# Moving the block-mask step ahead of the weight masking on VectorE, and ahead of the small transfers on GpSimd

## The chip, the cores and the metric

One Trainium2 chip, all 8 cores, each running the same program on its own 2048 of the 16384 tokens. Nothing is exchanged between cores. The time is the device time of the slowest core, in microseconds (us).

## The reference

Two layers follow each other on `x` of shape (2, 8192, 4096):

```python
def _L0_attn_ref(data, weight, mask):
    block_mask = mask.reshape(nb, 32, kb, 32).astype(jnp.float32).sum(axis=(1, 3)) > 0
    elem_mask = jnp.repeat(jnp.repeat(block_mask, 32, axis=0), 32, axis=1)
    return jnp.einsum('bsk,nk->bsn', data, weight * elem_mask)

x = x + _layernorm(_L0_attn_ref(_layernorm(x), L0_attn_weight, L0_attn_mask))
x = x + _layernorm(einsum('bsi,oi->bso', _layernorm(x), sign(L0_ffn_weight)) + bias)
```

Both weights and the integer mask are 4096 x 4096. What this change touches is the block mask: every 32 x 32 block of the mask is summed, and a block of the first weight counts only if its sum is above zero.

## The kernel before

Each core works through its tokens in four chunks of 512 (`c` = 0 to 3), and in each chunk through two layers. A layer is 16 slabs: slab `sl` covers 512 output columns (`nsl = sl // 2`) and half of the contraction (`kh = sl % 2`). For one slab TensorE (PE) runs 64 matmuls of 512 columns (L474), 16 for each of four token tiles. After each odd slab the four accumulated banks are moved out of PSUM (in the first layer of chunk 0 by VectorE, DVE: L528, with statistics in L537).

In chunk 0 the weights come as 32-bit floats and have to be prepared. For each slab `emit_w_load_prep` (L338) makes SyncE (SP) load eight pieces of 512 KB into two alternating buffers `WST` (L364); a piece may be loaded only once the piece two before it has been used. In layer 0 DVE multiplies each piece by the block mask `BTE` into the slab buffer `WSL` (L393); there are two slab buffers. Then SP writes the finished slab, 2 MB, to DRAM for the later chunks (L418), ahead of the loads of the next slab in its queue. The preparation of slab `sl + 1` is issued before the matmuls of slab `sl`, so that the two overlap.

The block mask is built during the same stage, for one `nsl` at a time, in two steps:

- `emit_mask_front(nsl)` (L220), on GpSimd (POOL) alone: four loads of 2 MB of mask rows (L243), and for each a tree of five additions (L258) that leaves column sums. Even `nsl` works in `OS` and `MHI`, odd `nsl` in the two halves of `XP`.
- `emit_mask_tail(nsl)` (L267): ScalarE (ACT) converts the sums to `COLRED` (L280); PE sums over rows with one matmul into `ptB` (L292); DVE compares with zero into `BRT` (L306); PE transposes it in four small pieces (L297); DVE copies the result to `BT` (L310); POOL writes `BT` to DRAM and reads it back, spread over the partitions, into one of two buffers `BTE` (L323, L332).

`front` 0 and 1, `tail` 0 and 1, and `front` 2 and 3 come before the first slab. After that, at each even slab `sl = 2j`, the program issues `tail(j + 2)` and `front(j + 4)`. `tail(j + 2)` waits on POOL for `bte_freed[j]`, the masking of slab `2j + 1`. Every engine runs its own instructions strictly in the order of the program; only semaphores tie the engines together. The lines around the change:

```python
for sl in range(NSL):
    if sl + 1 < NSL:
        nxt = emit_w_load_prep(c, layer, sl + 1)
    ...
    emit_slab_mm(c, layer, sl, ready, su, ev_at, ht_mark, site, ...)
    if c == 0 and layer == 0 and sl % 2 == 0:
        j = sl // 2
        if j + 2 <= 7:
            emit_mask_tail(j + 2, False)
        if j + 4 <= 7:
            emit_mask_front(j + 4)
```

Of the kernel before, what the change touches and what calls it, by code (L numbers as in the profile page):

```python
# [15 lines left out]
BF16 = mybir.dt.bfloat16  # L16
# [21 lines left out]
def build():  # L38
# [16 lines left out]
    with es:  # L55
        def sb(name, shape, dt):
            return es.enter_context(nc.sbuf_tensor(name, shape, dt))
# [11 lines left out]
        BRT = sb("BRT", [4, 512], BF16)  # L69
        BT = sb("BT", [128, 128], BF16)  # L70
# [13 lines left out]
        ptB = es.enter_context(nc.psum_tensor("ptB", [128, 1024], F32))  # L84

        sem = {n: es.enter_context(nc.semaphore(n)) for n in SEMS}
        cnt = {n: 0 for n in SEMS}

        def inc(ins, n, k=1):
            cnt[n] += k  # L90
            ins.then_inc(sem[n], k)
            return (n, cnt[n])

        def wt(eng, marker):
            if marker is None:
                return
            n, v = marker
            if v > 0:
                eng.wait_ge(sem[n], v)

        blk = es.enter_context(nc.Block())
# [9 lines left out]
        bte_freed = {}  # L111
# [6 lines left out]
        @blk.gpsimd  # L118
        def _(g):
            g.dma_start(IDN[:, :], idn_d[:, :]).then_inc(sem["sA"], 16)  # L120
            g.dma_start(P4T[:, :], p4_d[:, :]).then_inc(sem["sA"], 16)
            g.dma_start(ONES1[:, :], ones1_d[:, :]).then_inc(sem["sA"], 16)
            g.dma_start(OS[0:1, :], bias_d[:, :]).then_inc(sem["sA"], 16)
# [96 lines left out]
        def emit_mask_front(nsl):  # L220
# [14 lines left out]
            def _(g):  # L235
# [28 lines left out]
                        cur = tree[:, dst_off:dst_off + dst_n]  # L264
                halv[nsl] = ("vPs", cnt["vPs"])

        def emit_mask_tail(nsl, first):  # L267
            halv = mask_halv
            conv = mask_conv
            par = nsl % 2  # L270
            XPI = XP[:, :].bitcast(I32)
            tree = MHI if par == 0 else XPI[:, 4096:8192]
            fin_base = 3072

            @blk.scalar
            def _(s):
                wt(s, halv[nsl])
                if nsl >= 1:
                    s.wait_ge(sem["vTp"], 5 * (nsl - 1) + 1)
                ins = s.activation(COLRED[:, :],  # L280
                                   tree[:, fin_base:fin_base + 512],
                                   AF.Identity)
                conv[nsl] = inc(ins, "vAs", 1)

            @blk.tensor
            def _(t):
                wt(t, conv[nsl])
                if first:
                    wt(t, bias_ptB_free)
                if nsl >= 1:  # L290
                    t.wait_ge(sem["vMk"], 2 * (nsl - 1) + 1)
                ins = t.matmul(ptB[0:4, 0:512], P4T[:, :], COLRED[:, :],  # L292
                               start=True, stop=True)
                inc(ins, "vTp", 1)
                t.wait_ge(sem["vMk"], 2 * nsl + 1)
                for r in range(4):
                    ins = t.transpose(ptB[:, :].bitcast(BF16)[:, 1024 + r * 4:  # L297
                                                              1028 + r * 4],
                                      BRT[0:4, r * 128:(r + 1) * 128],
                                      IDN[0:4, 0:4])  # L300
                    inc(ins, "vTp", 1)

            @blk.vector
            def _(v):
                v.wait_ge(sem["vTp"], 5 * nsl + 1)
                ins = v.tensor_scalar(BRT[0:4, :], ptB[0:4, 0:512], 0.0, None,  # L306
                                      OP.is_gt)
                inc(ins, "vMk", 1)
                v.wait_ge(sem["vTp"], 5 * nsl + 5)
                ins = v.tensor_copy(BT[:, 16 * nsl:16 * nsl + 16],  # L310
                                    ptB[:, :].bitcast(BF16)[:, 1024:1040])
                inc(ins, "vMk", 1)

            res = {}

            @blk.gpsimd
            def _(g):
                g.wait_ge(sem["vMk"], 2 * nsl + 2)
                g.wait_ge(sem["sB"], cnt["sB"])
                if nsl >= 2:  # L320
                    wt(g, bte_freed[nsl - 2])
                bteb = BTE[nsl % 2]
                g.dma_start(btd_d[:, :], BT[:, 16 * nsl:16 * nsl + 16]  # L323
                            ).then_inc(sem["sB"], 16)
                cnt["sB"] += 16
                g.wait_ge(sem["sB"], cnt["sB"])
                for a in range(4):
                    out_ap = bass.AP(bteb[:, :].tensor, 32 * a * 512,
                                     [[512, 32], [16, 32], [1, 16]])
                    in_ap = bass.AP(btd_d[:, :].tensor, a * 16,  # L330
                                    [[0, 32], [64, 32], [1, 16]])
                    g.dma_start(out_ap, in_ap).then_inc(sem["sB"], 16)  # L332
                    cnt["sB"] += 16
                res["m"] = ("sB", cnt["sB"])

            bte_ready[nsl] = res["m"]
# [469 lines left out]
        for c in range(NCH):  # L806
            t0 = c * TC
            if c == 0:
                emit_p0_part1(0, list(range(NT)), phase="loads")
                emit_mask_front(0)  # L810
                emit_mask_front(1)
                emit_mask_tail(0, True)
                emit_mask_tail(1, False)
                emit_mask_front(2)
                emit_mask_front(3)
                emit_p0_part1(0, list(range(NT)), phase="stats")
            else:
                emit_p0_part1(c, [1, 2, 3])
            p0_norm = emit_p0_part2(c)
            a2_norm = None  # L820

            for layer in range(2):
                ev_at = {}
                site = 1 if layer == 0 else 3
                norm_marks = p0_norm if layer == 0 else a2_norm
                single_pt = (c == 0 and layer == 0)
                te_done = {}
                tr_base = state["tr_groups"]

                def pre_tt(t, tt, _nm=norm_marks, _sp=single_pt, _c=c,  # L830
                           _layer=layer, _te=te_done):
                    extra = []
                    if _c == 0 and _layer == 1 and tt == 0:
                        extra.append(("vMk", 16))
                    for grp in range(2):
                        _te[(tt, grp)] = emit_h_transposes_grp(
                            t, tt, grp, _nm[tt] if grp == 0 else None,
                            _sp, extra if grp == 0 else [])

                def ht_mark(tt, _tb=tr_base):  # L840
                    return ("vTe", _tb + 2 * tt + 2)

                pend = emit_w_load_prep(c, layer, 0)
                for sl in range(NSL):
                    if sl + 1 < NSL:
                        nxt = emit_w_load_prep(c, layer, sl + 1)
                    if layer == 0 and fin_pending[0] is not None:
                        fc, fev = fin_pending[0]
                        if sl == 0:
                            fin_chain[0] = emit_finalize_chain(fc, fev)  # L850
                        elif sl == 1:
                            for ftt in range(NT):
                                emit_finalize_tile(fc, fin_chain[0], ftt)
                            fin_pending[0] = None
                    ready, su = pend
                    emit_slab_mm(c, layer, sl, ready, su, ev_at, ht_mark, site,
                                 pre_tt=pre_tt if sl == 0 else None)
                    if c == 0 and layer == 0 and sl % 2 == 0:
                        j = sl // 2
                        if j + 2 <= 7:  # L860
                            emit_mask_tail(j + 2, False)
                        if j + 4 <= 7:
                            emit_mask_front(j + 4)
                    if layer == 1 and sl == 8 and c + 1 < NCH:
                        emit_p0_part1(c + 1, [0])
                    if sl + 1 < NSL:
                        pend = nxt

                prev_ev[0] = {tt: ev_at[(7, tt)] for tt in range(NT)}

                if layer == 0:
                    a2_norm = emit_a2(c, t0, ev_at)
                else:
                    fin_pending[0] = (c, ev_at)
# [45 lines left out]
```

## Time and profile before

| | us |
|---|---|
| median of two runs | 3415.11 |
| lowest and highest of the two | 3378.73, 3451.49 |
| the profiled execution | 3383.73 |
| its span on the slowest core, core 3 | 3382.2 |
| spans of all cores | 3337.3 to 3382.2 |
| busy in the span: PE, DVE, ACT, POOL | 2033.5, 889.0, 606.0, 356.1 |

The profile is of one execution. Its times count from the first instruction of core 3. The page gives PE a busy share of 60%, but the slices of the span differ: the stage that the change touches, layer 0 of chunk 0, lies between about 220 and 865 us, and there PE is busy a third of the time or a little more. POOL is hardly used after 740 us.

### The profile page before, as it was taken

Reading aid. Unit: us, or ns where it says so; the run is one execution under the profiler, and the core shown is the slowest. Engines: PE = TensorE matmul, PEld = TensorE weight load, DVE = VectorE, ACT = ScalarE, POOL = GpSimd, SP = SyncE. Lnnn points to the kernel's source line nnn. Section 1 sums busy time; section 2 is a strip of 40 time slices with the busy share of each in tenths; the row PEclk is TensorE's granted clock in tenths of the full one; section 3 lists DMA queues with packets and bytes.
Section 4 is the critical chain, followed back from the end, with each engine's and each line's share of the span. In section 5 each row is a group of like instructions: output and inputs, shape, how many; then the busy total and the mean of one; then the engine's idle time right before and its main releaser. Section 6 shows DMA issues by size and latency. Waiting matters only on the chain.

```text
span 3382.2 us, 24252 instructions; the slowest of 8 cores (3337.3 to 3382.2 us)
## 1 busy us (share of the span) xinstructions
PE 2033.5 (60%) x9272; PEld 935.3 (28%) x9272; DVE 889.0 (26%) x1300; ACT 606.0 (18%) x460; POOL 356.1 (11%) x296
## 2 busy tenths in 40 slices
PE   1013333345235545455994899589579966966992
PEld 0011111112112212222442444234234432433441
DVE  0043444434401011024004122410312142022214
ACT  0130000000443232241114200211330030125000
POOL 3554444400000000000000000000000000000000
PEclk9997766678667777777996999889779987986996
DMA  3367766766356666655343344444334444442442
GB/s 125 123 253 216 242 223 238 242 214 221 114 159 189 199 193 200 200 190 175 149 149 129 120 179 156 163 167 156 132 117 164 160 149 174 149 153 74 156 157 107
DMA packets 72947, 573.15 MB, mean 169 GB/s; under 512 B 8800, under 2 KB 8816, under 8 KB 42112
## 3 DMA queue, kind: packets, MB, share of 16 engines
q1 hardware_dynamic: 58752, 444.62, 38.2%
q0 software_dynamic: 14080, 126.97, 11.3%
q8 instruction: 75, 1.23, 0.1%
q14 instruction: 40, 0.33, 0.0%
HBM read 470.86 MB, written 100.70 MB: 169 GB/s over the span
## 4 chain that ended last, share of the span: by engine, by line
PE 37%; DMA 34%; DVE 11%; ACT 11%; issue 4%; POOL 1%; SPq 0%; DVEq 0%; ACTq 0%; POOLq 0%
PE pmm L474 36%; DMA WST<-w1s 13%; DMA WST<-w2s 11%; DVE WSL L393 4%; DMA out<-OS 3%; DMA XS<-x 3%; ACT WSL L407 2%; ACT HS L738 2%; ACT HS L707 2%; DVE OS L786 2%; ACT HT L214 1%; DMA WSL<-c1m 1%; DVE BNST L593 1%; DMA OS<-mask 1%; PE ptA L204 1%
## 5 line engine op out<-in xcount | busy, mean ns | idle before, releaser
L474 PE MATMUL pmm<-WSL,HT 128*128 128x512 bf16 x8192 | 1904.8, 397 | 648.9 <-ACT WSL L407 260.1
L474 PEld LDWEIGHTS pmm<-WSL,HT 128*128 128x128 bf16 x8192 | 826.7, 102 | 1717.8 <-issue 839.2
L530 DVE TENSOR_TENSOR ARAW<-pmm,BIASF 128x512 bf16<-128x512 f32 x128 | 88.6, 692 | 1021.0 <-PE pmm L474 1021.0
L393 DVE TENSOR_TENSOR WSL<-WST,BTE 128x1024 bf16<-128x1024 f32 x128 | 234.3, 1849 | 348.1 <-DMA WST<-w1s 332.4
L204 PE MATMUL ptA<-IDN,HS 128*128 128x128 bf16 x576 | 64.7, 301 | 367.3 <-ACT HS L738 235.5
L511 DVE BATCH_NORM_STATS2 BNST<-ARAW 128x6 f32<-128x512 bf16 x96 | 59.3, 681 | 544.2 <-ACT ARAW L501 544.2
L407 ACT ACTIVATE WSL<-WST 128x1024 bf16<-128x1024 f32 x128 | 133.4, 1054 | 166.4 <-DMA WST<-w2s 166.2
L204 PEld LDWEIGHTS ptA<-IDN,HS 128*128 128x128 bf16 x576 | 56.6, 139 | 380.7 <-issue 380.0
L258 POOL TENSOR_TENSOR XP<-XP 128x2048 int32<-128x2048 int32 (+4 forms) x80 | 137.7, 1721 | 104.9 <-DMA XP<-mask 97.2
L675 POOL DMA_DIRECT2D XS<-x x32 | 22.4, 699 | 1129.8 <-DVE XP L700 1080.9
L562 POOL DMA_DIRECT2D XS<-x x24 | 12.7, 528 | 1161.9 <-ACT HS L627 1093.9
L214 ACT ACTIVATE HT<-ptA 128x2048 bf16<-128x2048 bf16 x36 | 67.6, 1877 | 274.5 <-PE ptA L204 274.5
L280 ACT ACT_TABLE_LOAD x8 | 10.3, 1283 | 555.3 <-POOL XP L258 283.7
L501 ACT ACTIVATE ARAW<-pmm 128x512 bf16<-128x512 f32 x96 | 57.3, 597 | 266.9 <-PE pmm L474 153.1
L593 DVE BATCH_NORM_STATS2 BNST<-XS 128x6 f32<-128x512 f32 x128 | 78.4, 679 | 101.5 <-DMA XS<-x 101.5
L501 ACT ACT_TABLE_LOAD x24 | 30.8, 1283 | 403.5 <-PE pmm L474 403.5
L537 DVE BATCH_NORM_STATS2 BNST<-ARAW 128x6 f32<-128x512 bf16 x160 | 98.9, 681 | 4.1
L297 PE MATMUL ptB<-IDN,BRT 4*128 4x4 bf16 x32 | 1.9, 161 | 139.6 <-DVE BRT L306 139.6
L258 POOL TENSOR_TENSOR MHI<-MHI 128x1024 int32<-128x1024 int32 (+1 forms) x64 | 76.1, 1189 | 7.7
L786 DVE SCALAR_TENSOR_TENSOR OS<-XP,AUX,OS 128x4096 f32<-128x4096 bf16 x16 | 71.8, 4485 | 1.7
L292 PE MATMUL ptB<-COLRED,P4T 128*4 128x512 bf16 x8 | 3.4, 430 | 114.0 <-ACT COLRED L280 114.0
L258 POOL TENSOR_TENSOR MHI<-OS 128x2048 int32<-128x2048 int32 x16 | 57.5, 3596 | 111.5 <-DMA OS<-mask 111.5
(57 smaller groups left out, 742.2 us busy)
## 6 DMA issues: line engine op xcount, KB each, us to landing
WSL<-c1m SPq DMA_DIRECT2D x48, 2048.0 KB, 7.9
WSL<-c2m SPq DMA_DIRECT2D x48, 2048.0 KB, 7.8
WST<-w1s SPq DMA_DIRECT2D x128, 512.0 KB, 6.4
WST<-w2s SPq DMA_DIRECT2D x128, 512.0 KB, 4.4
XS<-x POOLq DMA_DIRECT2D x56, 1024.0 KB, 5.5
OS<-mask POOLq DMA_DIRECT2D x16, 2048.0 KB, 10.2
XP<-mask POOLq DMA_DIRECT2D x16, 2048.0 KB, 10.0
c1m<-WSL SPq DMA_DIRECT2D x16, 2048.0 KB, 8.8
```

Of the source, the lines that this page charges most:

```text
L204: ins = t.transpose(pt[:, j * 128:(j + 1) * 128], HS[:, ktg * 128:(ktg + 1) * 128], IDN[:, :])
L214: ins = eng.activation(dst, src, AF.Identity)
L258: ins = g.tensor_tensor(tree[:, dst_off:dst_off + dst_n], a[:, :, 0], a[:, :, 1], op=OP.add)
L393: ins = v.tensor_tensor(dst, src, mk, op=OP.mult)
L407: ins = s.activation(buf[:, j0 * 512:(j0 + KTQ) * 512], WST[(wfirst + q) % 2][:, :], AF.Sign)
L474: ins = t.matmul(acc_bank(use8, nsl, tt), st_ap, mv_ap, start=(kh == 0 and j == 0), stop=(kh == 1 and j == KTS - 1))
L501: ins = s.activation(dst, acc_bank(use8, nsl, tt), AF.Identity)
L530: ins = v.tensor_tensor(dst, acc_bank(use8, nsl, tt), BIASF[:, nsl * 512:(nsl + 1) * 512], op=OP.add)
L537: ins = v.bn_stats(BNST[:, sslot * 48 + nsl * 6: sslot * 48 + (nsl + 1) * 6], ARAW[:, tt * D + nsl * 512: tt * D + (nsl + 1) * 512])
L593: ins = v.bn_stats(bn[:, (hf * 4 + q) * 6: (hf * 4 + q + 1) * 6], xb[:, q * 512:(q + 1) * 512])
L707: ins = s.activation(HS[:, :], XP[:, tt * D:(tt + 1) * D], AF.Square, accum_out=XSQ[:, tt:tt + 1])
L786: ins = v.scalar_tensor_tensor(OS[:, :], XP[:, tt * D:(tt + 1) * D], mrs3, OS[:, :], OP.subtract, OP.add)
```

## The change

The two DVE instructions of the mask tail (the comparison and the copy) become a function of their own, `emit_mask_tail_pre`. At an even slab `sl = 2j` it is now issued first, for `nsl = j + 2`; `emit_mask_front(j + 4)` comes right behind it; both stand ahead of the preparation of slab `sl + 1`. The rest of the tail (ACT, PE, POOL) stays behind the matmuls of slab `sl`. POOL's wait for `bte_freed` is written out as a constant of the same value. No instruction is added or taken away.

```diff
+        def emit_mask_tail_pre(nsl):
+            @blk.vector
+            def _(v):
+                v.wait_ge(sem["vTp"], 5 * nsl + 1)
+                ins = v.tensor_scalar(BRT[0:4, :], ptB[0:4, 0:512], 0.0, None,
+                                      OP.is_gt)
+                inc(ins, "vMk", 1)
+                v.wait_ge(sem["vTp"], 5 * nsl + 5)
+                ins = v.tensor_copy(BT[:, 16 * nsl:16 * nsl + 16],
+                                    ptB[:, :].bitcast(BF16)[:, 1024:1040])
+                inc(ins, "vMk", 1)
+
         def emit_mask_tail(nsl, first):
...
-            @blk.vector
-            def _(v):
-                v.wait_ge(sem["vTp"], 5 * nsl + 1)
-                ins = v.tensor_scalar(BRT[0:4, :], ptB[0:4, 0:512], 0.0, None,
-                                      OP.is_gt)
-                inc(ins, "vMk", 1)
-                v.wait_ge(sem["vTp"], 5 * nsl + 5)
-                ins = v.tensor_copy(BT[:, 16 * nsl:16 * nsl + 16],
-                                    ptB[:, :].bitcast(BF16)[:, 1024:1040])
-                inc(ins, "vMk", 1)
...
                 if nsl >= 2:
-                    wt(g, bte_freed[nsl - 2])
+                    g.wait_ge(sem["vW"], 16 * nsl - 16)
...
                 emit_mask_front(0)
                 emit_mask_front(1)
+                emit_mask_tail_pre(0)
+                emit_mask_tail_pre(1)
                 emit_mask_tail(0, True)
...
                 for sl in range(NSL):
+                    if c == 0 and layer == 0 and sl % 2 == 0:
+                        j = sl // 2
+                        if j + 2 <= 7:
+                            emit_mask_tail_pre(j + 2)
+                        if j + 4 <= 7:
+                            emit_mask_front(j + 4)
                     if sl + 1 < NSL:
                         nxt = emit_w_load_prep(c, layer, sl + 1)
...
-                    if c == 0 and layer == 0 and sl % 2 == 0:
-                        j = sl // 2
-                        if j + 2 <= 7:
-                            emit_mask_tail(j + 2, False)
-                        if j + 4 <= 7:
-                            emit_mask_front(j + 4)
+                    if c == 0 and layer == 0 and sl % 2 == 0 and sl // 2 + 2 <= 7:
+                        emit_mask_tail(sl // 2 + 2, False)
```

How this changes the order on DVE, at the start of the stage. Before, DVE masks slab 0 and slab 1 (eight L393 each), does the mask step of `nsl` 2, and masks slab 2:

```order
L393 TENSOR_TENSOR WSL<-WST,BTE 128x1024 x8
L374 UNCONDITIONAL_BRANCH
L393 TENSOR_TENSOR WSL<-WST,BTE 128x1024 x8
L303 UNCONDITIONAL_BRANCH
L306 TENSOR_SCALAR BRT<-ptB 4x512
L310 COPY BT<-ptB 128x16
L374 UNCONDITIONAL_BRANCH
L393 TENSOR_TENSOR WSL<-WST,BTE 128x1024 x8
```

After the change the same rows of DVE read (line numbers are those of the changed kernel, L394 is the masking, L271 and L275 the mask step):

```order
L394 TENSOR_TENSOR WSL<-WST,BTE 128x1024 x8
L268 UNCONDITIONAL_BRANCH
L271 TENSOR_SCALAR BRT<-ptB 4x512
L275 COPY BT<-ptB 128x16
L375 UNCONDITIONAL_BRANCH
L394 TENSOR_TENSOR WSL<-WST,BTE 128x1024 x8
L375 UNCONDITIONAL_BRANCH
L394 TENSOR_TENSOR WSL<-WST,BTE 128x1024 x8
```

The mask step has moved from behind the masking of slab 1 to ahead of it. The same happens at slabs 3, 5, 7, 9 and 11.

On POOL, before, the end of `front(3)` (its last tree, in `XP`) is followed by the transfers of `tail(2)`, and then by `front(4)`, whose first load goes to `OS`:

```order
L258 TENSOR_TENSOR XP<-XP 128x256
L258 TENSOR_TENSOR XP<-XP 128x128
L316 UNCONDITIONAL_BRANCH
L323 DMA btd<-BT 128x16
L332 DMA BTE<-btd 32x32x16 x4
L234 UNCONDITIONAL_BRANCH
L243 DMA OS<-mask 128x4096
```

After the change, the end of `front(3)` is followed at once by `front(4)`:

```order
L258 TENSOR_TENSOR XP<-XP 128x256
L258 TENSOR_TENSOR XP<-XP 128x128
L234 UNCONDITIONAL_BRANCH
L243 DMA OS<-mask 128x4096
L258 TENSOR_TENSOR MHI<-OS 128x2048
```

and the transfers of `tail(2)` (L324, L333) stand behind the last tree of `front(4)`, ahead of `front(5)`:

```order
L258 TENSOR_TENSOR MHI<-MHI 128x128
L317 UNCONDITIONAL_BRANCH
L324 DMA btd<-BT 128x16
L333 DMA BTE<-btd 32x32x16 x4
L234 UNCONDITIONAL_BRANCH
L243 DMA XP<-mask 128x4096
```

So each `front` from 4 to 7 has moved ahead of one set of small transfers. The order on PE, ACT and SP is as before.

## Rows read from the trace of the kernel before

**Rows 1.** Waits, 300 to 700 us: waiter <- releaser, total us, times, longest us

```profile
DVE WSL L393 <- DMA WST<-w1s: 205.2, 49, 12.2
...
PE ptB L297 <- DVE BRT L306: 124.9, 5, 27.4
...
POOL btd L323 <- DVE BT L310: 46.2, 5, 9.7
```

**Rows 2.** Timeline of DVE around slabs 2 and 3 (start us, duration us, idle before)

```profile
353.29 2.47 DVE L528 CAST ARAW<-pmm 128x512 bf16<-128x512 f32 x4
...
370.56 4.96 DVE L393 TENSOR_TENSOR WSL<-WST,BTE 128x1024 bf16<-128x1024 f32 x2 [12.22 <-DMA WST<-w1s]
...
396.65 0.67 DVE L306 TENSOR_SCALAR BRT<-ptB 4x512 bf16<-4x512 f32 x1
```

**Rows 3.** Timeline of PE: the matmuls of slab 2, and each mask matmul (L292)

```profile
274.21 0.38 PE L292 MATMUL ptB<-COLRED,P4T 128*4 128x512 bf16 x1
...
354.12 15.64 PE L474 MATMUL pmm<-WSL,HT 128*128 128x512 bf16 x64 [36.41 <-DVE ARAW L528]
369.69 0.38 PE L292 MATMUL ptB<-COLRED,P4T 128*4 128x512 bf16 x1
...
461.72 0.38 PE L292 MATMUL ptB<-COLRED,P4T 128*4 128x512 bf16 x1
...
552.72 0.38 PE L292 MATMUL ptB<-COLRED,P4T 128*4 128x512 bf16 x1
...
641.86 0.38 PE L292 MATMUL ptB<-COLRED,P4T 128*4 128x512 bf16 x1
...
713.60 0.38 PE L292 MATMUL ptB<-COLRED,P4T 128*4 128x512 bf16 x1
```

**Rows 4.** Timeline of DVE: first masking instruction of slabs 1, 5, 7

```profile
272.44 1.45 DVE L393 TENSOR_TENSOR WSL<-WST,BTE 128x1024 bf16<-128x1024 f32 x1 [13.96 <-DMA WST<-w1s]
...
459.89 3.86 DVE L393 TENSOR_TENSOR WSL<-WST,BTE 128x1024 bf16<-128x1024 f32 x2 [9.65 <-DMA WST<-w1s]
...
549.64 3.21 DVE L393 TENSOR_TENSOR WSL<-WST,BTE 128x1024 bf16<-128x1024 f32 x2 [9.53 <-DMA WST<-w1s]
```

**Rows 5.** The same for slabs 9 and 11

```profile
639.03 3.58 DVE L393 TENSOR_TENSOR WSL<-WST,BTE 128x1024 bf16<-128x1024 f32 x2 [9.39 <-DMA WST<-w1s]
...
705.89 2.36 DVE L393 TENSOR_TENSOR WSL<-WST,BTE 128x1024 bf16<-128x1024 f32 x2 [4.45 <-DMA WST<-w1s]
```

**Rows 6.** Timeline of PE, then DVE: an undisturbed mask tail

```profile
147.26 0.59 PE L292 MATMUL ptB<-COLRED,P4T 128*4 128x512 bf16 x1 [53.67 <-ACT COLRED L280]
...
149.15 0.17 DVE L310 COPY BT<-ptB 128x16 bf16<-128x16 bf16 x1 [0.52 <-PE ptB L297]
```

**Rows 7.** Timeline of POOL: tail(2), first load and last row of front(4), end of front(7)

```profile
302.24 0.56 POOL L323 DMA_DIRECT2D btd<-BT  x1 [9.73 <-DVE BT L310]
...
315.43 0.57 POOL L243 DMA_DIRECT2D OS<-mask  x1
...
382.75 6.76 POOL L258 TENSOR_TENSOR MHI<-MHI 128x1024 int32<-128x1024 int32 x4
...
646.62 10.69 POOL L258 TENSOR_TENSOR XP<-XP 128x2048 int32<-128x2048 int32 x5 [3.75 <-DMA XP<-mask]
```

**Rows 8.** Timeline of DVE: evictions after slabs 8, 12 and 14

```profile
624.59 2.47 DVE L528 CAST ARAW<-pmm 128x512 bf16<-128x512 f32 x4
...
761.73 2.48 DVE L528 CAST ARAW<-pmm 128x512 bf16<-128x512 f32 x4
...
817.96 2.48 DVE L528 CAST ARAW<-pmm 128x512 bf16<-128x512 f32 x4
```

**Rows 9.** Instructions by line, window 223:665, then window 697:850 (busy us, mean ns)

```profile
L393 DVE TENSOR_TENSOR WSL<-WST,BTE 128x1024 bf16<-128x1024 f32 x80 | 176.1, 2224 | 239.5 <-DMA WST<-w1s 223.9 <-DMA btd<-BT 15.4 <-issue 0.2
...
L393 DVE TENSOR_TENSOR WSL<-WST,BTE 128x1024 bf16<-128x1024 f32 x40 | 48.6, 1225 | 87.0 <-DMA WST<-w1s 87.0
```

**Rows 10.** Stage 370:397 (PE, PEld, DVE, ACT, POOL busy, granted clock, DMA share, GB/s)

```profile
370.00:397.00 27.00, 0.07 (x1) 0.00 (x0) 17.04 (x9) 1.91 (x2) 16.00 (x10) 0.59 0.58 196
```

## The prediction

> **What bounds the kernel now.** The change reaches only layer 0 of chunk 0, so I read the waits of 300 to 700 us first. The largest in time that looks like the change's target is PE's: its transposes of the mask waited 124.9 us for DVE's comparison, up to 27.4 us at a time, and POOL waited 46.2 us for DVE's copy [rows 1]. DVE itself waited 205.2 us for weight pieces [rows 1]. Which of them ends last is seen in the timelines. DVE masks slab 3 until 396.6, and does the comparison at 396.65 [rows 2]; PE had stood ready with its mask matmul since 369.69 [rows 3]. But what PE wants next is the matmuls of slab 3, and these need the masked slab, which is ready at the same 396.6. PE's long wait is thus for the slab, under another name: the comparison costs it about 1 us. The stage is bound by the chain on each weight piece: SP's load, DVE's masking, which frees the buffer, SP's next load. PE and POOL hang beside it.
>
> What the masking costs depends on POOL. Its instruction takes 2224 ns on average while POOL builds trees, 1225 ns without [rows 9]. Three pairs of slabs with a front beside each last from the evictions at 353.29 to those at 624.59, 90.4 us each [rows 2, 8]; a pair without a front lasts 56.2 us, from 761.73 to 817.96 [rows 8]. So a front costs the chain some 34 us, by its loads and its trees together.
>
> **The wait that is added.** DVE's comparison of `nsl` j + 2 now stands ahead of the masking of slab 2j + 1, but it still needs PE's mask matmul, which stands behind all 64 matmuls of slab 2j. Before, DVE masked slab 2j + 1 beside these matmuls; now eight maskings queue behind the comparison, behind them SP's loads from the third piece on (two are in the buffers), and then PE's slab 2j + 1. So DVE may start a slab no sooner than the end of the slab before on PE, plus the tail. I compare that with when it started before. An undisturbed tail goes from the mask matmul's start at 147.26 to the end of the copy at 149.32, 2.06 us, with a matmul of 0.59 us [rows 6]; with the 0.38 us of this stage [rows 3] it is 1.85. The mask matmul's start plus 1.85, less the old first masking:
>
> - slab 1: 274.21 + 1.85 - 272.44 = 3.6 [rows 3, 4]
> - slab 3: 369.69 + 1.85 - 370.56 = 1.0 [rows 2, 3]
> - slab 5: 461.72 + 1.85 - 459.89 = 3.7 [rows 3, 4]
> - slab 7: 552.72 + 1.85 - 549.64 = 4.9 [rows 3, 4]
> - slab 9: 641.86 + 1.85 - 639.03 = 4.7 [rows 3, 5]
> - slab 11: 713.60 + 1.85 - 705.89 = 9.6 [rows 3, 5]
>
> The sum is 27.5 us. The delays are small because the matmuls of a slab take only 15.6 us [rows 3], and the first piece of the next slab arrives late anyway: 12.22 us of idle DVE before slab 3 [rows 2], behind the 2 MB that SP writes back first. At slab 11, where no front runs, it arrives sooner and the new wait shows more. A delayed first masking delays the third load by as much, and so the whole chain; nothing in the stage catches up, since DVE is idle waiting for pieces. Slab 9 will be free of fronts after the change (below), and would then look like slab 11: 5 us more. Against that, of the 13.2 us on slabs 1 to 7 a part is given back: POOL goes on while DVE stands still, and a front's work in that time costs no masking. At 34 us of cost in 90 us that is about 5. I keep 27.5.
>
> **The waits that go.** PE has done its transposes early and starts odd slabs at the last masking, some 1 us sooner. This is worth nothing: the next slab on the chain waits for DVE and the loads, not for PE.
>
> POOL no longer waits for the comparison at the end of a front. `front(4)` starts at the end of `front(3)`, 302.24 - 9.73 = 292.5, and not at 315.43 [rows 7]: 23 us sooner. With the other waits, POOL's 46.2 us in all [rows 1], `front(7)` ends near 610 and not at 657.3 [rows 7]. What is late next? The transfers of `tail(2)`, now behind `front(4)`: 292.5, plus that front's 389.5 - 315.4 = 74.1, plus 13.2 for the transfers (302.24 to 315.43), is 380 [rows 7]. DVE needs `BTE` for slab 4 after 396.65 [rows 2], so 17 us remain, and later fronts gain distance. The `vW` wait in the tail is past by then. ACT's conversions have their sums earlier than before. So POOL is early and nobody waits for it: the direct gain is nothing.
>
> What its earliness does to the chain is not shown by the trace, and I bound it. If a front costs its 34 us whenever it runs, nothing changes; four fronts stay four fronts, only packed closer and over sooner. If instead a pair costs 90.4 us in POOL's company however dense that is, 46 us less of company saves 46 x 34 / 90.4 = 17 us. On the other side, today's fronts stand in step with the slabs: their quiet end falls on the end of the odd slabs. Today one tree of a front's four falls into the pause before an odd slab's first piece (DVE idle from 358.3 to 370.56 [rows 2]) and meets no masking. A front lengthens the 16 maskings of its pair by 2224 - 1225 = 1.0 us on average [rows 9], 16 us in all. If the fourth tree meets maskings like the other three, that grows by a third, 5 us a front, 21 us for four. I take 0, the middle of -17 and +21.
>
> The Trainium skill ("SBUF — State Buffer", Who interferes with whom) states a rule that speaks against the packing: a VectorE instruction with two inputs in SBUF and a GpSimd instruction that reads SBUF block each other for the whole instruction. The trace agrees that the masking, which is such an instruction, grows from 1225 to 2224 ns [rows 9]. By that rule the sum would lean to its upper end of +21; by the pairs' additive cost it stays at 0.
>
> **Sum.** 3383.7 (the profiled execution) + 27.5 - 0 + 0 = 3411; leaning a little on the refund of 5 us, I say 3408. The median of the two runs shown, 3415, lies between two values 73 us apart, and the profiled execution is close to the lower; I count from the profile. The change is +0.7%, inside the 2% (68 us) that a measurement of this kernel can tell from no change.
>
> **Rivals.**
>
> - Packing pays. POOL is done 46 us sooner and the slabs behind it run at 56 us a pair, while the new waits vanish beneath late pieces: with POOL loading masks without a pause, first pieces may arrive at every odd slab as late as at slab 3, where the wait is 1.0 us. Then 6 x 1 - 17 gives -11: 3373. Against it: at slabs 9 and 11 no front runs, and their 4.7 and 9.6 us are certain.
> - PE's old wait was real. If the 124.9 us were on the path, five waits of 25 us would go: 3383.7 - 125 = 3259. Against it stand [rows 2, 3]: the end of the wait coincides with the end of the slab's masking.
> - PE's clock, the one on the slower side. DVE now waits for each even slab's matmuls, so their speed is on the path. They took 15.6 us even after 36.41 us of idle [rows 3]. While PE idles the granted clock is 0.59, near the lower level of 1.2 GHz [rows 10]. If the bursts stayed there, 64 matmuls would take between 0.59 / 0.38 = 1.55 times as long (the mask matmul in either state [rows 3, 6]) and twice, 8.6 to 15.6 us more. Six slabs add 52 to 94 us to the 27.5: about +100, 3484. It decides (over 2%) as soon as the bursts take over 22 us. Against it: PE's pattern of bursts and pauses is nearly unchanged, and the bursts of this stage are fast. The Trainium skill ("TensorE: Matmul & The Clock Gate", Loop structure matters more than you think) says that a long wait for data sends PE to its lower clock. The idle row agrees [rows 10], but the burst behind such a wait is fast here [rows 3], which keeps this rival's chance low.
> - Late mask. If `front(4)`, in the company of slabs 1 and 2 and of the write-back, took 30 us more than 74, `BTE` would come 13 us after slab 4 wants it, and DVE would stand. Once behind, POOL's period sets the pace: up to four times 13, +80 with the 27.5, 3463. Against it: the 17 us of room, and that POOL gains on the slabs each time.
>
> **Chances.** The waits as summed: 0.70, with a range of its own from 3390 (27.5 - 17, less 5) to 3437 (27.5 + 21 + 5). Packing pays: 0.17. PE's old wait real, faster by over 2%: 0.03. The clock: 0.05. Late mask: 0.05, of which half is beyond 2%. So faster 0.03, same 0.89, slower 0.08. The range goes from 3373, the packing rival, to 3445, the upper end with the spread of the runs added.
>
> **What would show it.** In the changed profile: DVE idle before the first masking of slabs 1, 3, 5, 7, 9 and 11 is put down to PE's small matmuls or DVE's copy, 16 to 19 us after the last slab's end; PE's wait at the transposes is gone, and an equal one stands before the odd slabs' matmuls; `front(7)` ends near 610; the last eviction of layer 0 comes some 27 us later. A pair of slabs with a front much under 90 us would prove the packing rival; a first masking that waits for BTE, the late mask; bursts above 20 us, the clock. The forecast is wrong if the layer ends earlier than before or over 60 us later.

## The result, and the profile after

| | before | after |
|---|---|---|
| median, us (runs) | 3377.34 (23) | 3395.46 (24) |
| lowest, us | 3362.97 | 3384.51 |
| ratio of the runs, 95% interval | | 1.0075 [1.0054, 1.0096] |
| profiled execution: span of the slowest core | 3382.2 (core 3) | 3391.5 (core 1) |
| mean of the eight spans | 3354.7 | 3378.6 |

The change costs 0.75%, 25 us, and the interval keeps clear of no change. In some executions the cores of one die show a lower granted clock and end later; the medians above include them, the ratios leave them out, and so the ratio stands for means of about 3373 and 3398 us, 25 apart, where the medians lie 18 apart. The slowest cores of the two profiled executions differ by 9 us only, the means of all cores by 24. Spans of the cores lie up to 45 us apart in one of these two, so where a few microseconds matter, the following reads all eight. The interval is 0.2% to either side: a difference well under the 2% that the prediction named can be told.

First the waits between 300 and 700 us in the kernel after (waiter <- releaser, total us, times, longest), against [rows 1]:

```profile
DVE WSL L394 <- DMA WST<-w1s: 186.3, 46, 14.8
PE pmm L475 <- DVE WSL L394: 155.6, 5, 41.8
...
POOL btd L324 <- DVE WSL L394: 86.1, 3, 58.6
...
DVE BRT L271 <- PE ptB L304: 48.8, 4, 12.9
...
PE ptB L309 <- DVE BRT L271: 3.7, 4, 0.9
```

PE's 124.9 us at the mask transposes have become 3.7. What stands there instead is a longer wait for the masked slab, 155.6 us, which was hidden under the other name before. DVE has a wait that it did not have: 48.8 us for PE's mask matmul here, and 78.3 us over the whole stage, by the group of its line between 220 and 900 us (busy us, mean ns, idle before):

```profile
L271 DVE TENSOR_SCALAR BRT<-ptB 4x512 bf16<-4x512 f32 x6 | 4.1, 679 | 78.3 <-PE ptB L304 78.3
```

At slab 11, where no front runs, the timelines of DVE and of PE show the step whole. They answer to the last rows of [rows 3, 5].

```profile
720.39 2.48 DVE L529 CAST ARAW<-pmm 128x512 bf16<-128x512 f32 x4
722.98 2.47 DVE L538 BATCH_NORM_STATS2 BNST<-ARAW 128x6 f32<-128x512 bf16 x4
738.55 0.68 DVE L271 TENSOR_SCALAR BRT<-ptB 4x512 bf16<-4x512 f32 x1 [13.10 <-PE ptB L304]
739.74 0.17 DVE L275 COPY BT<-ptB 128x16 bf16<-128x16 bf16 x1 [0.51 <-PE ptB L309]
740.05 2.36 DVE L394 TENSOR_TENSOR WSL<-WST,BTE 128x1024 bf16<-128x1024 f32 x2
```

```profile
721.22 16.91 PE L475 MATMUL pmm<-WSL,HT 128*128 128x512 bf16 x64 [15.85 <-DVE ARAW L529]
738.06 0.38 PE L304 MATMUL ptB<-COLRED,P4T 128*4 128x512 bf16 x1
739.37 0.23 PE L309 MATMUL ptB<-IDN,BRT 4*128 4x4 bf16 x4 [0.93 <-DVE BRT L271]
760.28 16.16 PE L475 MATMUL pmm<-WSL,HT 128*128 128x512 bf16 x64 [20.67 <-DVE WSL L394]
```

DVE has masked slab 10 and moved the banks of slab 9 out of PSUM (the eviction) by 725.5, and stands for 13.1 us, until PE has finished the 64 matmuls of slab 10. Then two maskings follow each other without a gap (2.36 us for both): both pieces had been lying in their buffers. From the eviction's start to the first masking it is 19.7 us. Before, that eviction began at 696.38 (timeline of DVE of the kernel before),

```profile
696.38 2.48 DVE L528 CAST ARAW<-pmm 128x512 bf16<-128x512 f32 x4
```

and the first masking of slab 11 at 705.89 [rows 5], 9.5 us later. That is the 10 us of one slab.

POOL's side, from its timeline (end of `front(3)`, start of `front(4)`, transfers of `tail(2)`, end of `front(7)`), against [rows 7]:

```profile
283.61 9.70 POOL L258 TENSOR_TENSOR XP<-XP 128x2048 int32<-128x2048 int32 x5 [7.73 <-DMA XP<-mask]
293.87 0.55 POOL L243 DMA_DIRECT2D OS<-mask  x1 [0.56 <-POOL XP L258]
...
363.25 0.56 POOL L324 DMA_DIRECT2D btd<-BT  x1 [0.74 <-POOL MHI L258]
...
596.74 0.40 POOL L258 TENSOR_TENSOR XP<-XP 128x128 int32<-128x128 int32 x1 [0.43 <-POOL XP L258]
620.77 0.57 POOL L324 DMA_DIRECT2D btd<-BT  x1 [23.63 <-DVE WSL L394]
```

`front(7)` ends at 597.1 instead of 657.3, 60 us sooner, and then POOL stands for 23.6 us until slab 7 is masked and `BTE` may be overwritten. In this profile nobody waits for POOL.

The time by slab says where the 25 us arise. Below is when each slab is masked (the start of SP's write-back of it, read from the eight timelines and averaged, us); the runs beside it are those of the next section:

| kernel | 0 | 1 | 3 | 5 | 7 | 8 | 9 | 10 | 11 | 15 |
|---|---|---|---|---|---|---|---|---|---|---|
| before | 259 | 299 | 392 | 482 | 573 | 621 | 662 | 695 | 724 | 847 |
| after | 258 | 310 | 419 | 516 | 610 | 641 | 679 | 710 | 749 | 873 |
| dve_only | 262 | 302 | 399 | 493 | 587 | 638 | 679 | 711 | 749 | 877 |
| pool_only | 257 | 308 | 419 | 516 | 607 | 638 | 668 | 701 | 731 | 856 |
| pe_early | 260 | 313 | 422 | 518 | 607 | 638 | 669 | 701 | 731 | 855 |
| nofront_before | 262 | 303 | 367 | 429 | 490 | 522 | 552 | 585 | 615 | 740 |
| nofront_after | 257 | 299 | 369 | 439 | 509 | 541 | 579 | 612 | 650 | 776 |
| nofront_pe_early | 258 | 299 | 362 | 424 | 485 | 517 | 548 | 580 | 610 | 734 |

Each line is one profiled execution, so that differences of a few us between lines decide nothing alone. The kernel after ends the layer 26 us late, and nearly all of that is still there at the end of the program (24 us in the mean span). On the way it is not spread evenly. Up to slab 7 it falls behind by 37 us, gets 22 of them back by slab 10, and loses 10 again at slab 11.

### The profile page after: what moved, and what is told of

It reads as the page before. It is cut to its first block, busy times and chain, and to the rows that moved or that the text cites. A ratio compares the mean times of both kernels' runs of the same rounds, so it can differ in the third digit from the quotient of the medians.

```text
span 3391.5 us, 24252 instructions; the slowest of 8 cores (3359.4 to 3391.5 us)
## 1 busy us (share of the span) xinstructions
PE 2032.9 (60%) x9272; PEld 934.7 (28%) x9272; DVE 885.5 (26%) x1300; ACT 606.4 (18%) x460; POOL 347.9 (10%) x296
## 4 chain that ended last, share of the span: by engine, by line
PE 40%; DMA 31%; DVE 11%; ACT 11%; issue 4%; POOL 1%; SPq 0%; DVEq 0%; ACTq 0%; POOLq 0%
PE pmm L475 39%; DMA WST<-w1s 12%; DMA WST<-w2s 11%; DVE WSL L394 4%; DMA out<-OS 3%; ACT WSL L408 2%; DMA XS<-x 2%; ACT HS L739 2%; ACT HS L708 2%; DVE OS L787 2%; ACT HT L214 1%; DVE BNST L594 1%; DMA OS<-mask 1%; DMA WSL<-c1m 1%; PE ptA L204 1%
## 5 line engine op out<-in xcount | busy, mean ns | idle before, releaser
L394 DVE TENSOR_TENSOR WSL<-WST,BTE 128x1024 bf16<-128x1024 f32 x128 | 229.2, 1806 | 311.8 <-DMA WST<-w1s 310.4
L594 DVE BATCH_NORM_STATS2 BNST<-XS 128x6 f32<-128x512 f32 x128 | 78.3, 679 | 97.4 <-DMA XS<-x 97.4
L784 DVE TENSOR_SCALAR OS<-ARAW,RS 128x4096 f32<-128x4096 bf16 x16 | 37.7, 2353 | 122.2 <-DMA out<-OS 121.3
```

The costliest lines, as they stand in the source:

```text
L394: ins = v.tensor_tensor(dst, src, mk, op=OP.mult)
L594: ins = v.bn_stats(bn[:, (hf * 4 + q) * 6: (hf * 4 + q + 1) * 6], xb[:, q * 512:(q + 1) * 512])
```

## The experiments

Two theories. **W**: DVE's wait for the end of PE's even slab is the whole cost. **P**: the cost is the closer packing of POOL's fronts, and the wait lies beneath late pieces anyway. The ratios are all to the kernel before, timed beside each group of runs; a range in brackets is its 95% interval.

### One half each

`dve_only` is the changed kernel with `front` back behind the tail:

```diff
-                        if j + 4 <= 7:
-                            emit_mask_front(j + 4)
...
                         emit_mask_tail(sl // 2 + 2, False)
+                    if c == 0 and layer == 0 and sl % 2 == 0 and sl // 2 + 4 <= 7:
+                        emit_mask_front(sl // 2 + 4)
```

> Only the DVE half of the change: the mask step stands ahead of the masking of the odd slab, while POOL keeps its old order (the transfers of tail(j+2), then front(j+4)). Theory W (the added wait on PE is the whole cost): about +27 us over the kernel before, 0.8%, and a layer 0 of chunk 0 that ends 25 to 30 us later. Theory P (the packing of the fronts is the cost, and the wait lies beneath late pieces): under +8 us. In both, POOL waits for the masking of the odd slab (bte_freed) where it waited for the copy before, so its fronts do not start sooner.

`pool_only` is the kernel before with the two calls exchanged:

```diff
-                        if j + 2 <= 7:
-                            emit_mask_tail(j + 2, False)
                         if j + 4 <= 7:
                             emit_mask_front(j + 4)
+                        if j + 2 <= 7:
+                            emit_mask_tail(j + 2, False)
```

> Only the POOL half: front(j+4) is issued ahead of the transfers of tail(j+2); DVE and PE keep the order of before. Theory W: within 10 us of the kernel before, since four fronts cost the same wherever they run; front(7) ends about 45 us sooner. Theory P: +20 us or more. A third theory, that packing pays and is hidden in the full change by the waits: -10 to -17 us.

Measured: the DVE half 1.0061 [1.0038, 1.0085], 21 us; the POOL half 1.0006 [0.9981, 1.0031], 2 us. Together they make 0.67%, against 0.75% for the whole. The interval of `pool_only`, -6 to +11 us, keeps clear of P's +20 and of the -10 to -17 of the third theory, that packing pays; both fall. `front(7)` ended at 607.7 there, 50 us sooner than before. In the profile of `dve_only` the new wait has the size that it has in the whole change:

```profile
L271 DVE TENSOR_SCALAR BRT<-ptB 4x512 bf16<-4x512 f32 x6 | 4.1, 679 | 77.1 <-PE ptB L304 77.1
```

The table shows what packing does. In `pool_only` slab 7 is 34 us later than before, since most of the four fronts have run by then, and by slab 9 it is only 6 us later. The layer ends 9 us late in this one profile; the timing shows 2 us, and 9 lies inside its interval.

### The fronts taken away

Both kernels of this pair leave out the mask loads and trees of `front` 4 to 7, so that what they compute for the columns of `nsl` 4 to 7 is not the reference; they serve this comparison alone.

```diff
         def emit_mask_front(nsl):
             halv = mask_halv
+            if nsl >= 4:
+                halv[nsl] = ("vPs", cnt["vPs"])
+                return
```

> The kernel before without the mask loads and trees of column groups 4 to 7 (the block mask of these groups is then that of stale sums; the tails still run). Additive cost of 34 us a front: about -136 us, 4%. If the masking of a slab were not slowed by POOL and its loads, 0. Pairs of slabs then last about 56 us from slab 2 on.

> The changed kernel without the mask loads and trees of column groups 4 to 7, as in the run before this one. With no front in the way the first pieces of an odd slab land some 9.5 us before DVE may take them, at five slabs, and 3.6 us at slab 1: theory W expects +50 us against the kernel before without those fronts, twice what the full change costs. Theory P (packing costs) expects 0 to 10, since there is nothing left to pack.

Measured against the kernel before: 0.9636 [0.9603, 0.967] without the fronts, 0.973 [0.9693, 0.9767] with the change on top. The difference is 0.94% of 3390, 32 us, from four runs and three; with the two intervals taken as independent, 15 to 49 us. (A later expectation quotes 34 us, the difference of the medians.) The four fronts cost 3.64%, 123 us or 31 each, where I had 34. P's 0 to 10 us is missed; whether the change costs more without fronts than with them, 32 us against 25, the timing can't tell. W's 50 us is too high, though. The rows show why: the evictions behind the masking of slabs 8 and 10 stand in the timeline of DVE in `nofront_after`,

```profile
539.52 1.88 DVE L532 CAST ARAW<-pmm 128x512 bf16<-128x512 f32 x3
...
608.99 2.48 DVE L532 CAST ARAW<-pmm 128x512 bf16<-128x512 f32 x4
```

some 70 us apart (the first line shows the last three of four copies; the first began at 538.9), where a pair takes 61 to 63 us in `nofront_before` by the table. From slab 1 to slab 15 the change adds 477 - 437 = 40 us in these profiles: 8 us at each of five waits, not the 9.6 of slab 11, which I had taken over for all of them. Slab 1 costs nothing, where I had 3.6.

### The wait shortened

The clean test of W leaves DVE's new order alone and lets PE answer sooner. PE's part of the mask tail goes inside the even slab: the mask matmul after the first token tile, the transposes after the second. ACT's conversion is issued ahead of the slab. (Shown are the new PE function and its call; the old places of both parts are switched off.)

```diff
+        def pe_mask(t, nsl, step):
+            if step == 0:
+                wt(t, mask_conv[nsl])
+                t.wait_ge(sem["vMk"], 2 * (nsl - 1) + 1)
+                ins = t.matmul(ptB[0:4, 0:512], P4T[:, :], COLRED[:, :],
+                               start=True, stop=True)
+                inc(ins, "vTp", 1)
+            else:
+                t.wait_ge(sem["vMk"], 2 * nsl + 1)
...
                     if kh == 1 and tt < NT - 1:
                         mm_marks[tt] = inc(ins, "vMM", 1)
+                    if mask_nsl is not None and tt < 2:
+                        pe_mask(t, mask_nsl, tt)
```

> The changed kernel, with PE's part of the mask tail moved into the even slab: the mask matmul after the first 16 of its 64 matmuls, the transposes after the second 16. DVE's mask step can then end some 8 us after the slab starts, before the first piece of the next slab lands (9.5 to 17 us). Theory W: the whole 25 us vanish, and the time is that of the POOL half alone, within 0.3% of the kernel before. If the cost lay in anything else of DVE's new order than the end of PE's matmuls, +0.6 to 0.8% stays. POOL's waits for the masking of the odd slab stay as in the changed kernel.

> The DVE half alone (POOL in its old order), with PE's mask matmul and transposes inside the even slab, after 16 and 32 of its 64 matmuls. The DVE half alone took 0.61% more. Theory W: that goes back to 0, within 0.3% of the kernel before. If 0.4% or more stays, DVE's wait for the end of PE's slab isn't what the half costs.

> The changed kernel without the mask loads and trees of column groups 4 to 7 (stale sums there, the tails still run), with PE's part of the tail inside the even slab. Without fronts the change cost 34 us, 0.9%. Theory W: with the early PE part the time is that of the kernel before without those fronts, 0.964 of the kernel before, within 0.3%; layer 0 of chunk 0 ends as early, its pairs of slabs at 60 to 61 us and not at 70.

| | without early PE part | with it |
|---|---|---|
| whole change | 1.0075 [1.0054, 1.0096] | 1.0021 [0.9987, 1.0055] |
| DVE half | 1.0061 [1.0038, 1.0085] | 1.0017 [0.9983, 1.0051] |
| change without fronts (against 0.9636 before) | 0.973 [0.9693, 0.9767] | 0.9643 [0.9581, 0.9705] |

In each case what stays can't be told from nothing. The drop itself, the two intervals taken as independent, is 0.54% with an uncertainty of 0.40 in the first line, 0.44 with 0.41 in the second and 0.87 with 0.72 in the third: each is clear of nothing by little, and the three agree. In `pe_early` DVE's idle time before the comparison falls from 78.3 to 14.2 us:

```profile
L271 DVE TENSOR_SCALAR BRT<-ptB 4x512 bf16<-4x512 f32 x6 | 4.1, 679 | 14.2 <-PE ptB L296 14.2
```

while the copy behind it now waits 18.5 us for PE's transposes, where it waited 3.1: together 33 us instead of 81. The timeline of its DVE at slab 3 has the order that I wanted: the mask step is over before the first piece lands, and DVE waits for that piece.

```profile
369.02 0.68 DVE L271 TENSOR_SCALAR BRT<-ptB 4x512 bf16<-4x512 f32 x1 [1.40 <-PE ptB L296]
372.78 0.17 DVE L275 COPY BT<-ptB 128x16 bf16<-128x16 bf16 x1 [3.08 <-PE ptB L302]
375.09 1.23 DVE L427 TENSOR_TENSOR WSL<-WST,BTE 128x1024 bf16<-128x1024 f32 x1 [2.14 <-DMA WST<-w1s]
```

The table by slab agrees: `nofront_pe_early` ends the layer at 734 after a start at 258, 476 us; `nofront_before` takes 478; `nofront_after` takes 519. So the cost comes from DVE's wait for the end of PE's slab; a remainder from something else in DVE's new order could be up to 0.5% by the intervals, and the profiles without fronts show none. The profile of `dve_pe_early` fits less well: its layer ends at 865 after a start at 262, 603 us, against 615 in `dve_only` and 588 before, with single cores ending from 851 to 884. Its timing, +0.17% and at most 0.51%, is the better measure, since it has six executions; the profile alone would leave 15 of the 27 us open.

### The chain of pieces

If the chain of load, masking and next load is what bounds the stage, more pieces in flight should shorten it more than any order of the mask step does. `HS` is idle during the weight stages of chunk 0 and holds two more pieces:

```diff
...
+        HSF = HS[:, :].bitcast(F32)
+        WP = [WST[0][:, :], WST[1][:, :], HSF[:, 0:1024], HSF[:, 1024:2048]]
...
-                        prior = u - 2
+                        prior = u - 4
...
+                        if sl == 0 and u % 4 >= 2 and q < 4:
+                            s.wait_ge(sem["vTr"], 8 * (layer + 1))
-                        sn = "sW%d" % (u % 2)
-                        s.dma_start(WST[u % 2][:, :],
+                        sn = "sW%d" % (u % 4)
+                        s.dma_start(WP[u % 4],
...
```

> The kernel before with four buffers for weight pieces instead of two (the two new ones lie in HS, which is idle during the weight stages), so that four loads are in flight. If the chain of piece load, masking and next load bounds the two weight stages of chunk 0, each slab gets shorter: from 29 us to about 22 us without a front, at 6 MB a slab and the 300 GB/s that the busiest stretches show, and by less with a front: 100 to 200 us in all, 3 to 6%. If the DMA rate bounds the stages already, 0.

> The same four buffers in the changed kernel. Theory W: while DVE stands behind PE's matmuls, the loads now run on for four pieces instead of two, so part of the lost time is caught up; but the pace of the rest is faster, so that the 16 us of PE's matmuls plus 2 of the tail weigh against a shorter slab. I expect +10 to +40 us against the kernel before with four buffers. Were the wait harmless, the two would agree.

> Four buffers, with PE's part of the tail early as in the first run of this group. Theory W: as fast as the kernel before with four buffers, or 10 us faster, since neither PE nor DVE waits for the other at the mask step; it should be the fastest of all.

| four buffers in | ratio to the kernel before | slab 15 masked at, us |
|---|---|---|
| the kernel before | 0.9358 [0.9297, 0.9418] | 759 |
| the kernel after | 0.9381 [0.9331, 0.943] | 774 |
| the kernel after, PE's part early | 0.9343 [0.9282, 0.9403] | 766 |

The number of pieces in flight is what bounds the two weight stages: 6.4% go, 217 us, a little over what I had expected, and the alternative, that the DMA rate was the bound already, falls. The stage of layer 1 between 1000 and 1200 us, on core 3 in the kernel before and with four buffers (PE, PEld, DVE, ACT, POOL busy, granted clock, DMA share, GB/s):

```profile
1000.00:1200.00 200.00, 97.75 (x384) 40.40 (x384) 15.72 (x24) 59.85 (x56) 0.00 (x0) 0.72 0.65 195
```

```profile
1000.00:1200.00 200.00, 137.39 (x540) 56.61 (x539) 28.12 (x51) 81.49 (x78) 0.00 (x0) 0.83 0.80 272
```

195 GB/s become 272, and PE gets through 540 matmuls instead of 384. Over all eight cores it is 194 to 213 GB/s before and 268 to 276 with four buffers. The three versions with four buffers can't be told apart by their times, with two or three runs behind each ratio: the change costs 0.23%, 8 us, with an uncertainty of some 26, so that my 10 to 40 us is neither borne out nor missed. By slab, in one profile each, the change ends the layer 15 us later. With four buffers a rival comes true that I had given 0.05, the late mask. DVE of `ring4_after` waits for `BTE` before slabs 4, 6, 8 and 10:

```profile
390.43 1.23 DVE L398 TENSOR_TENSOR WSL<-WST,BTE 128x1024 bf16<-128x1024 f32 x1 [15.79 <-DMA BTE<-btd]
...
476.68 2.36 DVE L398 TENSOR_TENSOR WSL<-WST,BTE 128x1024 bf16<-128x1024 f32 x2 [18.86 <-DMA BTE<-btd]
...
555.08 2.36 DVE L398 TENSOR_TENSOR WSL<-WST,BTE 128x1024 bf16<-128x1024 f32 x2 [21.13 <-DMA BTE<-btd]
...
631.18 2.36 DVE L398 TENSOR_TENSOR WSL<-WST,BTE 128x1024 bf16<-128x1024 f32 x2 [17.14 <-DMA BTE<-btd]
```

Slabs are now as fast as fronts, and a mask that stands behind the next front comes late. `ring4_pe_early` has the same waits (73.5 us) without DVE's for PE and ends the layer at 766; the order of before, with the transfers first, has no wait of this size by the name of `BTE` (single ones of 10 us or less) and ends at 759. I had expected `ring4_pe_early` to be the fastest of all; its median, 3159.41, is the lowest, but within the spread. Since the times rank none of the three, the kernel before with four buffers is the one to take: it needs no new order and ends the layer first in its profile.

## Why the prediction was right or wrong

**The mechanism held.** I forecast that DVE's comparison would stand until PE's slab ends, and that this costs 27.5 us of 3383.7, with nothing gained elsewhere: +0.7% as the text says it. Measured is +0.75%, 25 us. `dve_only`, `pool_only` and the early PE part show it to be that wait. That the size fits so closely is in part luck, since the terms below miss in both directions.

**The step that failed is the first term of the sum.** It is "3383.7 (the profiled execution)", with "I count from the profile". That one execution lay above what the kernel before takes: 23 runs have a median of 3377.34, 6 us less, and the mean behind the ratio is about 3373, 11 us less. So the forecast of 3408, 24 us above the profiled execution, lies 13 us over the measured median of 3395.46. Worse, it lies below the only median that I had, 3415.11; beside that one it reads as 0.2% faster, and the kernel became slower. Of a median of two values 73 us apart only the lower one was any use, and the direction had to be stated as a ratio.

**The terms by slab.** The term of slab 11, 9.6 us, is right: slab 11 takes 39 us after slab 10 in the kernel after and 29 before. Slab 9 was entered at 4.7, with the remark that it would be free of fronts and cost 5 more. So it is: from slab 8 to 9 the kernel after takes 38 us and `pool_only` 30, and 8 is what it costs. The four terms under fronts, 13.2 us for slabs 1, 3, 5 and 7, are borne out where POOL keeps its old order: up to slab 7 `dve_only` takes 587 - 262 = 325 us, the kernel before 573 - 259 = 314, 11 more. With the packed fronts they shrink: at slab 7 `after` (610) is 3 us behind `pool_only` (607), so the refund of 5 us was too small, about 10 being right. And "nothing in the stage catches up" does not hold there. The first and the last masking row of slab 3 on DVE, first in the kernel after, then in `pool_only`, show a late start that is made up:

```profile
383.20 1.23 DVE L394 TENSOR_TENSOR WSL<-WST,BTE 128x1024 bf16<-128x1024 f32 x1
...
417.16 7.28 DVE L394 TENSOR_TENSOR WSL<-WST,BTE 128x1024 bf16<-128x1024 f32 x2 [6.14 <-DMA WST<-w1s]
```

```profile
378.51 1.23 DVE L393 TENSOR_TENSOR WSL<-WST,BTE 128x1024 bf16<-128x1024 f32 x1 [8.88 <-DMA BTE<-btd]
...
418.02 7.27 DVE L393 TENSOR_TENSOR WSL<-WST,BTE 128x1024 bf16<-128x1024 f32 x2 [7.37 <-DMA WST<-w1s]
```

The first masking is 4.7 us later, and the last ends at 424.4 against 425.3. In both, the last rows are pairs of slow maskings, 3.6 us each, beside one tree of POOL each, which would fit that POOL's trees set the pace there. No run tests this. At the end of the layer `after` is 17 us behind `pool_only`, and `pool_only` 9 behind the kernel before in its profile, 2 in its timing. How the 25 us split between 17 to 23 for the wait and the small rest for packing the runs leave open.

**The waits that go** were worth nothing, as forecast. PE's transposes waited 124.9 us before and 3.7 after, and the time rose. POOL was done 60 us sooner, and `pool_only` shows that to cost 2 us, with an interval of 8 us to either side. The bounds of -17 and +21 us for packing held, and 0 was the value. The Trainium skill's rule on instructions that block each other ("SBUF — State Buffer", Who interferes with whom) would have leaned to +21; that they block is seen here too, in maskings of 3.6 us beside a tree against 1.2 alone, but the packing did not lengthen the masking on the whole: it took 1806 ns on average from 220 to 900 us, against 1849 before. `front(7)` ended at 597, sooner than the 610 I gave. That sum had two slips: the 46.2 us hold a fifth wait, 8.6 us, that comes behind `front(7)`, and one set of transfers, 13.2 us, moves behind it too; 607 is what the rows give. The rest is mostly in the fronts themselves, 274 us for the four instead of 282.

**The rivals.** Packing pays: fell. PE's old wait real: fell. The clock: each of PE's bursts in this stage took 15.4 to 16.9 us after pauses of up to 41.8, and 15.3 to 16.9 in the kernel before, so they ran as fast; fell. Late mask: absent with two buffers, present with four. (Single waits of DVE by the name of `BTE` stand in some profiles with two buffers too, as at 378.51 above, 12 us at most; at 378.51 the `BTE` of slab 3 had been filled before the first slab, and the transfer named is that for slab 4.)

## What to carry to other kernels

A long wait by name is no cost if what the engine needs next arrives at the same moment: look at what ends last, not at who is named (PE's 124.9 us here). Before an instruction is moved up on an engine that runs strictly in order, look at where its own input stands on the other engine; a consumer that is moved ahead without its producer turns work that ran beside that producer into work behind it. Where a chain of small loads through two buffers paces a stage, try idle memory of a later stage as further buffers before a new order of what stands beside it: here it gave 6.4%, and the new order nothing. Write a forecast of under 1% as a ratio, and do not take its base from one execution.

## What the runs showed that I had not expected

Waits of 78 us on DVE cost 21 to 25 us of time. In the whole change some 18 of them arise at two of the six places, those without trees on POOL beside them (slabs 9 and 11, 8 and 10 us); beside packed fronts, up to slab 7, a late start cost 3 us in all. And two more buffers of 512 KB brought the rate of layer 1's weight stage on core 3 from 195 to 272 GB/s: a DMA share of 0.65 was no sign that the stage was near its limit.
